# Attention A: TensorE takes scores and value products two tiles at a time in place of one

## The reference

```python
qkv = x @ Wqkv.T + bqkv                      # x is layer-normed
q, k, v = heads(qkv)                         # b, 16, 1024, 8
q, k = apply_rope(q), apply_rope(k)
logits = einsum('bhid,bhjd->bhij', q, k) * SCALE
logits = einsum('bhij,gh->bgij', logits, Wpre)
attn = softmax(logits, axis=-1)
attn = einsum('bhij,gh->bgij', attn, Wpost)
out = einsum('bhij,bhjd->bhid', attn, v)
return out @ Wout.T + bout
```

## Time and profile before

| | |
|---|---|
| time of the profiled execution | 2200.29 us |
| its span | 2198.3 us |
| instructions | 61531 |
| stretch of attention A's tile loop | about 69 to 1455 us |
| busy: PE, DVE, ACT, POOL (share of span) | 94%, 86%, 79%, 40% |

### The profile page before, as it was taken

How to read it: one execution, slowest core, us unless ns; L and a number is a source line. 1 busy time by engine, 2 the same in 40 slices (tenths; PEclk the granted TensorE clock), 3 DMA queues, 4 the chain that set the end, 5 groups by cost and what they waited for, 6 DMA issues and landing times. The chain is left out here.

```text
span 2198.3 us, 61531 instructions
## 1 busy us (share of the span) xinstructions
PE 2076.9 (94%) x24854; PEld 1424.6 (65%) x24854; DVE 1901.0 (86%) x2598; ACT 1732.0 (79%) x3088; POOL 876.2 (40%) x958
## 2 busy tenths in 40 slices
PE   6799999999999999999999999978879999999977
PEld 3477777777777777777777777755536666655654
DVE  6899999999999999999999999958578888888694
ACT  3699999999999999999999999943357777777623
POOL 3333323332332333233333333344007777777640
PEclk9999999999999999999999999988989999999989
DMA  3599999999999999999999999950141111111001
GB/s 104 107 200 196 197 197 203 195 197 199 197 196 195 198 201 197 198 198 198 195 196 202 196 194 201 196 117 1 39 137 31 31 31 31 31 31 31 20 1 39
DMA packets 1088842, 303.72 MB, mean 138 GB/s; under 512 B 1062064, under 2 KB 1081904, under 8 KB 1088304
## 3 DMA queue, kind: packets, MB, share of 16 engines
q1 hardware_dynamic: 1087696, 299.33, 75.0%
q10 hardware_dynamic: 864, 0.47, 0.1%
HBM read 20.83 MB, written 10.49 MB: 14 GB/s over the span
## 5 line engine op out<-in xcount | busy, mean ns | idle before, releaser
L368 PE MATMUL a_out_ps<-a_vs,a_pT 128*128 128x128 f16 x4096 | 713.7, 219 | 5.3 <-DMA a_pT<-a_parts 5.3
L370 PE MATMUL a_out_ps<-a_vs,a_pT 128*128 128x128 f16 x4096 | 713.7, 219 | 0.0
L372 PE MATMUL a_out_ps<-a_vs,a_pT 128*128 128x128 f16 x4096 | 713.7, 219 | 0.0
L457 DVE SCALAR_TENSOR_TENSOR a_parts<-a_probs,a_parts 128x1024 f16<-128x1024 f32 x512 | 652.5, 1274 | 42.8 <-ACT a_parts L409 42.8
L401 ACT ACTIVATE a_probs<-a_score_ps,a_negmax 128x1024 f32<-128x1024 f32 x512 | 571.7, 1117 | 104.8 <-DVE a_negmax L451 96.1
L451 DVE TENSOR_REDUCE a_negmax<-a_score_ps 128x1 f32<-128x1024 f32 x512 | 622.6, 1216 | 25.8 <-PE a_score_ps L354 21.7
L511 POOL TENSOR_TENSOR a_weighed<-a_own_out,wpost 128x256 f32<-128x256 f32 x256 | 246.7, 964 | 940.8 <-DVE a_parts L457 932.4
L409 ACT ACTIVATE a_parts<-a_probs 128x1024 f16<-128x1024 f32 x512 | 540.5, 1056 | 0.0
L368 PEld LDWEIGHTS a_out_ps<-a_vs,a_pT 128*128 128x128 f16 x4096 | 401.3, 98 | 65.3 <-issue 4.2
L370 PEld LDWEIGHTS a_out_ps<-a_vs,a_pT 128*128 128x128 f16 x4096 | 401.3, 98 | 59.4
L350 PE MATMUL a_score_ps<-kh,a_qs 128*128 128x512 f16 x1024 | 389.8, 381 | 23.8 <-ACT a_probs L401 15.7
(11 more groups left out here) (233 smaller groups left out, 2226.1 us busy)
## 6 DMA issues: line engine op xcount, KB each, us to landing
b_qs<-q_parts SPq DMA_DIRECT2D x96, 64.0 KB, 1.9
b_ks<-k_parts SPq DMA_DIRECT2D x96, 64.0 KB, 1.9
a_pT<-a_parts SPq DMA_TRANSPOSE x256, 7.5
q_parts<-b_parts SPq DMA_DIRECT2D x32, 128.0 KB, 1.8
k_parts<-b_parts SPq DMA_DIRECT2D x32, 128.0 KB, 1.9
x<-x_dram SPq DMA_DIRECT2D x4, 512.0 KB, 7.9
a_rope<-rope_dram SPq DMA_DIRECT2D x1, 2048.0 KB, 10.6
out_dram<-x SPq DMA_DIRECT2D x4, 512.0 KB, 5.4
```

Of the source, the lines that this page charges most:

```text
L368: pe.matmul(out[:, 0:D], hi, vs[:, b, 0, j, :], start=j == 0, stop=False, skip_group_check=True)
L370: pe.matmul(out[:, 0:D], hi, vs[:, b, 1, j, :], start=False, stop=False, skip_group_check=True)
L372: last = pe.matmul(out[:, 0:D], lo, vs[:, b, 0, j, :], start=False, stop=j == JB - 1, skip_group_check=True)
L457: dve.scalar_tensor_tensor(out=parts[:, T % RING_H, 1, :], in0=probs[:, T % RING_P, :], scalar=PSCALE, in1=parts[:, T % RING_H, 0, :], op0 ...
```

## The change

TensorE's loop in `attend_a` steps by two: scores of tiles T + 8 and T + 9, then the value products of tiles T and T + 1. The instructions are the same ones, and no semaphore wait is added or removed; VectorE, ScalarE, GpSimd and SyncE keep their programs.

```diff
             for T in range(AH):
                 scores(T)
-            for T in range(TILES_A):
+            for T in range(0, TILES_A, 2):
                 scores(T + AH)
+                scores(T + AH + 1)
                 times_v(T)
+                times_v(T + 1)
```

## The result

The changed kernel took 2240.81 us (median of 3, 2239.97 to 2241.30) against 2201.43: a ratio of 1.0188, 95% interval 1.0174 to 1.0202. The profiled execution has a span of 2238.5 us against 2198.3, so 40.2 more; of that, 62 heads of 22.04 us in place of 21.42 are 38.4. The layers behind attention A didn't change: the last 738.5 us of this trace keep TensorE busy for 668.20 us, the last 738.3 of before for 669.06.

A forecast was written before the change was run, and what follows sets the result against it. TensorE sets the pace, VectorE 5% behind. Waits of 0.15 (tile 5) and 0.82 (tile 7) replace 0.33: a head 22.05 us for 21.42, 62 x 0.63 = 39 us; 2200.3 + 39 = 2239 profiled, median about 2240, range 2213 to 2257.

The forecast's parts named there:

- the start and end of the loop: Where value products begin, 0.94 us more once; at the end 0 to -1.3; both together taken as 0.
- The odd tile's slack: Score buffer of the odd tile, due 1.30 after the even one's while maxima stand 2.36 apart: slack from 1.26 to 0.20.
- `low_q` and `scale_q`: Mid-head steps on VectorE (1.19 us) and ScalarE (1.04), ahead of max(4) and high(1), in the chain worked to tiles 5 and 7.
- Nothing saved on TensorE: Between last score matmul and first value product: the 0.22 us is the matmul's own spacing, so no switch is saved.
- clock unchanged: TensorE's clock stays at 1.00 in the new gaps; the rival, a falling clock, adds 246 us, thus 2485; 1%.
- GpSimd beside a low: VectorE's low takes 1.45 us in place of 1.22 beside GpSimd's work; on low(4) it costs nothing.
- the rival at 2254: GpSimd's work slows low(2) in each head, putting max(5) and scores(7) 0.22 us later: 14 us more; 7%.
- The sum of TensorE's waits in the list: Profile after, TensorE's waits for exp (L401): near 60 us in place of 21.
- VectorE's idle time before tiles 0 and 2: VectorE idle for scores only before the maxima of tiles 0 (0.9 us) and 2 (0.65).
- the 0.33 at tile 6 of before: TensorE's wait per head before the change, read as late exp after delayed max(4); it goes, with later waits totalling 0.97.
- the first rival: Paired scores let VectorE get ahead and TensorE never waits: a head of 21.09 us, 2180 in total; 5%.
- the transposing DMA: Transposed parts land 7.5 us after the lows, over 3 us before the value products need them: cost nothing.

The follow-up runs named there:

- the other grouping: Against the kernel before: scores(T + 8), value products of T and T + 1, then scores(T + 9), two score buffers; 2277.44 us, ratio 1.0355.

## Why the prediction was right

- **The forecast** of 2240 met 2240.81. A head was to take 22.05 us and takes 22.04; tile 7 was to wait 0.82 and waits 0.80, tile 5 0.15 and 0.14, tile 6 not at all. It could be worked out this closely because one head is like the next, so that the steps read in one head of before hold for all 62. That the total met to 0.8 us is partly luck: the three runs of before lie 5.9 us apart, and the start and end of the loop had been put at nothing, where 1.8 of the 40.2 us stand outside the heads.
- **The odd tile's slack.** That two maxima stand 2.3 us apart whatever TensorE does, while their buffers are now due 1.30 apart, is shown three ways: a third buffer takes the price away, the other grouping (even tiles due early) raises the waits to 1.02 and 0.48 a head, and without `scale_q` and `low_q` there is none.
- **`low_q` and `scale_q`** as what uses the slack up: `low_q` taken away, `low_q` moved, `scale_q` taken away and `scale_q` moved, each with two buffers and the order of after, came within 3 us of the number worked out for them. Taken away together they came 7 and 9 us above it, in either order.
- **Nothing saved on TensorE, clock unchanged:** its 1.30 for the scores of a tile and 5.27 for a pair are those of before, and the granted clock stayed at 1.00 with a wait of 0.80 in each head of 22.04. In the kernel before it had been 0.50 from 63 to 73 us, around the 7.94 us that TensorE was idle ahead of its first scores, and not from 68 on only. The Trainium skill's rule on short idle times (TensorE: Matmul & The Clock Gate, "A second HAM failure mode") did not show here.
- **GpSimd beside a low** stayed on low(4), and cost nothing; the rival at 2254 didn't come about. It even became rarer: in before low(6) took 1.45 as well, now it takes 1.20.

Some things in it were off. The sum of TensorE's waits in the list was to be near 60 us; the distances give 62 x 0.94 = 58, but the list counts the weight loads' idle time, 98.7 us. At tile 7 that is 1.13 for a lateness of 0.80:

```profile
656.51 0.10 PEld L350 LDWEIGHTS a_score_ps<-kh,a_qs 128*128 128x128 f16 x1 [1.13 <-ACT a_probs L403]
```

The last weight load of scores(6) ended 1.13 before that, 0.33 before scores(7) would have been due. With two such waits in a head the list comes to 62 x (0.94 + 0.66) = 99. VectorE's idle time before tiles 0 and 2 was put at 0.9 and 0.65, and is 0.78 and 0.59.

Two more are larger, and didn't touch the forecast. The prediction read the 0.33 at tile 6 of before as a score buffer coming free late, and priced the first rival at 2180, as if 21.09 were within reach once that wait was gone. The three-buffer runs at 2202 show that it was not: the loop of VectorE and ScalarE held a head at 21.42. I had each step of that loop in the text, with its idle 0.66 before low(1), but not its closing.

And the transposing DMA was costed at nothing, from the 7.5 us to its landing alone; that SyncE's queue is held for about 5 us by each issue was not in the sum. For this change that was harmless (22.04 a head is well above 21.1), but not for the rival. In the runs at 2185 to 2190 (both without the two calls, and the two that have `scale_q` later and no wait for a buffer) the pairs are issued every 5.28 to 5.30 us and a head takes 21.12 to 21.18 on average. Over 62 heads that is 2 to 6 of the 4 to 9 us that they stand above the 2181 of TensorE alone. The rest lies outside these heads and stays open.

## What to carry to other kernels

With two buffers between a producer and an in-order consumer, look at the distance between the two deadlines: grouping the producer's work by two leaves each buffer its full round, yet takes slack from the second by as much as the consumer's own spacing exceeds the producer's. Work out the slack of each buffer separately, and then see which rare instruction (here one per eight tiles) falls into it. And a bounding engine that waits a little each period may only be keeping pace with a loop of the others: follow the chain round until it meets itself, before pricing what removing the wait would bring. Count the queue that issues the DMAs as one of these engines, though it is not in the list of busy time.

## What the hardware showed beyond that

The transposing DMA of 32 blocks of 128 x 128 in two bytes (two tiles, high and low parts) lands 6.7 to 9.2 us after its issue began, but what limited its rate was the issuing: 4.80 to 5.71 us of SyncE's queue for each, one behind the other, 5.21 us a pair with two engines waiting for the landings, and 5.28 to 5.30 in the four runs named above. Whether SyncE is at work for all of that time or is held back by what it feeds, no run shows. VectorE's and TensorE's rows of before don't tell of this bound, but SyncE's does, since a pair took 5.35 us there:

```profile
L331 SPq DMA_TRANSPOSE a_pT<-a_parts x256: 4800/5058/5831, 80.7 to 1444.5; - x128
```
